# A four-layer gated attention and expert kernel: the first attention layer's scores in two rounded passes, key norms' roots by iteration on GpSimd

## The reference

```python
def _L0_xattn_ref(x_query, x_context, Wq, Wkv, Wp, bp, ln_g, ln_b):   # 16 heads of 16
    q, k = layernorm(q, ln_g, ln_b), layernorm(k, ln_g, ln_b)         # per head, over its 16
    q = q * SCALE
    attn = jax.nn.softmax(jnp.einsum('bhqd,bhkd->bhqk', q, k), axis=-1)
    out = jnp.einsum('bhqk,bhkd->bhqd', attn, v)
    ...
x = x + jnp.tanh(g_xattn[0]) * _L0_xattn_ref(_layernorm(x, axis=-1), ctx_1024, ...)
x = x + jnp.tanh(g_ffn[0]) * _L0_ffn_ref(_layernorm(x, axis=-1), ...)
x = x + jnp.tanh(g_xattn[1]) * _L1_xattn_ref(_layernorm(x, axis=-1), ctx_1024, ...)
x = x + jnp.tanh(g_ffn[1]) * _L1_ffn_ref(_layernorm(x, axis=-1), ...)
```

## Time and profile before

| | us |
|---|---|
| median of three runs (584.68 to 585.03) | 584.78 |
| the profiled execution: its own time | 583.47 |
| its span in the trace | 581.6 |
| PE / PEld busy in it | 555.4 / 477.1 |
| DVE / ACT / POOL busy in it | 408.8 / 319.4 / 271.9 |
| granted PE clock, mean | 0.995 |

### The profile page before, as it was taken

One profiled execution on the slowest core, in us unless ns is written; L12 is line 12 of the kernel. 1 busy time (PEld: TensorE's weight loads), 2 busy tenths in 40 slices (PEclk: granted clock), 3 DMA queues, 4 the chain that ended last, 5 costly groups with the idle time before them and its releaser, 6 DMA issues.

```text
span 581.6 us, 13614 instructions
## 1 busy us (share of the span) xinstructions
PE 555.4 (95%) x5542; PEld 477.1 (82%) x5542; DVE 408.8 (70%) x831; ACT 319.4 (55%) x632; POOL 271.9 (47%) x237
## 2 busy tenths in 40 slices
PE   8999999999989999999999999998999999999994
PEld 8776667677657878888888888877899999979994
DVE  7877568578696666777767867767677677746652
ACT  3554555555664665566555556654465656636641
POOL 3755655765740164657567465731203233421424
PEclk9999999999999999999999999999999999999998
DMA  8910840000000000000000000019374567726112
GB/s 259 357 45 2 318 194 3 1 3 2 2 2 1 2 1 2 8 9 17 18 9 18 10 25 1 25 26 414 91 253 149 170 213 253 259 32 236 28 20 26
DMA packets 24091, 50.92 MB, mean 88 GB/s; under 512 B 7072, under 2 KB 17104, under 8 KB 20688
## 3 DMA queue, kind: packets, MB, share of 16 engines
q1 hardware_dynamic: 18560, 45.20, 21.4%
q0 software_dynamic: 4224, 3.70, 3.6%
q10 hardware_dynamic: 1232, 1.01, 0.6%
HBM read 37.89 MB, written 13.31 MB: 88 GB/s over the span
## 4 chain that ended last, share of the span: by engine, by line
PE 81%; DVE 7%; ACT 5%; POOL 4%; issue 2%; DMA 1%; POOLq 0%; DVEq 0%; ACTq 0%
PE ps L59 15%; PE ps L60 14%; PE ps L61 14%; PE ps L607 5%; PE ps L750 4%; PE ps L625 4%; PE ps L768 4%; PE ps L738 4%; ACT P L1642 3%; DVE KN L1140 3%; PE ps L641 3%; PE ps L515 2%; PE ps L816 2%; POOL P L1947 2%; PE ps L522 2%
## 5 line engine op out<-in xcount | busy, mean ns | idle before, releaser
L1947 POOL TENSOR_SCALAR P<-P,rinv 112x487 f32<-112x487 f32 x56 | 88.2, 1588 | 50.9 <-DVE rinv L1183 50.7
L1140 DVE TENSOR_REDUCE KN<-ps 112x4 f32<-112x1500 f32 x32 | 55.0, 1719 | 28.7 <-PE ps L607 28.6
L424 POOL DMA_INDIRECT out<-WS,rows_i x16 | 28.7, 1791 | 92.5 <-ACT WS L1789 89.0
L60 PE MATMUL ps<-XGf,WH 128*128 128x256 f32 x252 | 71.3, 283 | 0.0
L61 PE MATMUL ps<-XGf,WL 128*128 128x256 f32 x252 | 71.3, 283 | 0.0
L59 PE MATMUL ps<-XGf,WH 128*128 128x256 f32 x252 | 71.3, 283 | 0.0
L1886 POOL TENSOR_TENSOR sr<-sv,mhalf 125x32 f32<-125x32 f32 x13 | 70.7, 5435 | 1.1
L1521 DVE TENSOR_TENSOR WL<-WR,WH 128x1024 fp32r<-128x1024 f32 x48 | 57.1, 1219 | 13.6 <-ACT WH L1843 10.0
L1642 ACT ACTIVATE P<-ps 125x1344 f32<-125x1344 f32 x32 | 41.3, 1292 | 32.8 <-PE ps L625 32.8
L1705 ACT ACTIVATE P<-ps,nm 112x487 f32<-112x487 f32 x64 | 41.9, 664 | 31.7 <-DVE nm L1175 31.7
L1843 ACT ACTIVATE WH<-WR 128x1024 fp32r<-128x1024 f32 x48 | 48.7, 1049 | 0.1
(11 more groups left out here) (290 smaller groups left out, 1546.1 us busy)
## 6 DMA issues: line engine op xcount, KB each, us to landing
WR<-in_gupT SPq DMA_DIRECT2D x16, 1024.0 KB, 7.2
WR<-in_dwnT SPq DMA_DIRECT2D x8, 1024.0 KB, 10.3
xs<-ZT SPq DMA_DIRECT2D x14, 516.0 KB, 6.0
CT<-in_ctxT SPq DMA_DIRECT2D x1, 2250.0 KB, 11.1
P<-xs SPq DMA_DIRECT2D x7, 256.0 KB, 10.8
P<-xs SPq DMA_DIRECT2D x9, 128.0 KB, 2.6
Wk<-in_L_xattn_Wk SPq DMA_DIRECT2D x2, 512.0 KB, 11.1
Wv<-in_L_xattn_Wv SPq DMA_DIRECT2D x2, 512.0 KB, 11.1
```

The costliest lines, as they stand in the source:

```text
L60: e.matmul(out, ah, bl, start=False, stop=False)
L1140: e.tensor_reduce(heads(KN[b % 2][0:NQ, 3, :])[:, 4 * k:4 * k + 4, 16], ps[0:NQ, 0:4, 0:NC], AX.X, ALU.max, negate=True).then_inc(s("smax" ...
L1947: e.tensor_scalar(P[:, k, 0:487], P[:, k, 0:487], rinv[:, k:k + 1], None, ALU.mult).then_inc(s("psc"), 1)
```

## The change

The first layer's keys and queries are split. The keys of a head have mean zero over their 16 numbers, so the sixteenth is dropped: the queries' sixteenth is taken off the other fifteen (`qg` on POOL, and on the shift `Bt` in `gain`), and a head's 32 columns in `KN` now hold 15 rounded keys, the one (column 15, before 16), and 15 numbers that are the rest of the keys. The query tile holds its 15 numbers twice. `ksc` scales the keys in place in `kraw` and writes the queries twice; the new stage `khi` (ACT) writes the rounded part, the new stage `klo` (DVE for batch 0, POOL otherwise) the rest. `KT`, `QA`, `QB` become FR; `spqc` becomes two steps, ACT's rounded copy and DVE's difference `QL0`. `S0` and `st` each run two passes, the rounded queries and then `QL0`, both over the same `KT`, of single-pass FR products. All three `spkc` copies are ACT's. The keys' power on POOL becomes fourteen small instructions (`key_roots`). The planned times of nearly every stage of the first layer and of `FIRST1`, `EVEN`, `PREP1`, `TAIL1` and `WEIGHTS` are others; `TQ` and the second layer's work are as they were.

```diff
-QUAD = ((-0.96, "S0"), (0.14, "max0"), (4.29, "qt2"), (4.68, "qt2c"), (7.69, "st"), (9.09, "ex"), (10.12, "V0"))
+QUAD = ((-0.51, "S0"), (-0.76, "max0"), (4.6, "qt2"), (4.96, "qt2c"), (7.69, "st"), (9.24, "ex"), (10.64, "V0"))
...
+PREP = ((-37.73, "cs"), (-48.02, "norm", 0), (-30.8, "kp", 1, 0), (-31.59, "xt", 0), (-31.68, "xtc", 0),
+        (-28.84, "kp", 1, 1), (-28.38, "kq", 1), (-27.41, "kss", 1), (-24.74, "kp", 0, 0), (-22.83, "kp", 0, 1),
+        (-21.5, "kq", 0), (-19.22, "kss", 0), (-16.99, "qg"), (-19.73, "ksc", 1), (-20.33, "khi", 1),
+        (-26.62, "klo", 1), (-16.17, "spk", 0), (-15.24, "spkc", 0), (-15.1, "spk", 1), (-14.26, "spkc", 1),
+        (-11.21, "ksc", 0), (-6.81, "khi", 0), (-11.53, "klo", 0), (-15.34, "qaff"), (-5.28, "spq"), (-4.56, "spqc"),
+        (-3.45, "spk", 2), (-3.79, "spkc", 2))
...
                 elif stage == "spk":
-                    w.wait_ge(s("ksc"), o_("ksc", b, 0 if j == 2 else 1))
+                    w.wait_ge(s(f"klo{0 if j == 2 else 1}"), b + 1)
...
-                    for g in range(4):
+                    for v, g in itertools.product(range(2), range(4)):
                         rows = slice(32 * g, 32 * g + 32)
-                        t = e.matmul(ps[0:NQ, g, 0:NC], QA[b % 2][rows, k * NQ:(k + 1) * NQ], KT[b % 2][rows, k, 0:NC],
-                                     start=True, stop=True, tile_position=(32 * g, 0))
+                        t = e.matmul(ps[0:NQ, g, 0:376], (QA, QL0)[v][b % 2][rows, k * NQ:(k + 1) * NQ],
+                                     KT[b % 2][rows, k, :], start=(v == 0), stop=(v == 1), tile_position=(32 * g, 0))
...
-                    for j, g in itertools.product(range(3), range(4)):
+                    for j, v, g in itertools.product(range(3), range(2), range(4)):
                         rows = slice(32 * g, 32 * g + 32)
                         t = e.matmul(ps[0:125, g, j * NQ:(j + 1) * NQ], KT[b % 2][rows, k, j * 125:(j + 1) * 125],
-                                     QB[b % 2][rows, k * NQ:(k + 1) * NQ], start=True, stop=True,
+                                     (QB, QL0)[v][b % 2][rows, k * NQ:(k + 1) * NQ], start=(v == 0), stop=(v == 1),
                                      tile_position=(32 * g, 0))
...
-                    e.tensor_tensor(out_, kraw[:, p, :].rearrange("p (h d) -> p h d", d=16),
-                                    sr[:, p, :].unsqueeze(2).to_broadcast([125, 32, 16]), ALU.mult).then_inc(s("ksc"), 1)
+                    n = 32 if p else 16
+                    k = kraw[:, p, 0:16 * n].rearrange("p (h d) -> p h d", d=16)
+                    t = e.tensor_tensor(k, k, sr[:, p, 0:n].unsqueeze(2).to_broadcast([125, n, 16]), ALU.mult)
+                    if p == 0:
+                        q = kraw[0:NQ, 0, 256:512].rearrange("p (h d) -> p h d", d=16)[:, :, 0:15]
+                        t = e.tensor_tensor(query_twice(b), q.unsqueeze(2).to_broadcast([NQ, 16, 2, 15]),
+                                            sr[0:NQ, 0, 16:32].unsqueeze(2).unsqueeze(3).to_broadcast([NQ, 16, 2, 15]),
+                                            ALU.mult)
+                    t.then_inc(s("ksc"), 1)
...
-                elif stage == "spkc" and i[1] != 2:
-                    keys_copy(e, w, *i)
+                elif stage == "spqc":
+                    b, = i
+                    w.wait_ge(s("spqa"), b + 1)
+                    e.tensor_tensor(QL0[b % 2], ps[:, bank("spq", b), 0:448], f_(QA[b % 2]),
+                                    ALU.subtract).then_inc(bank_sem("spq", b), 1)
...
+            q = query_twice(b)
+            e.tensor_tensor(q, q, Bt.rearrange("p (h d) -> p h d", d=16)[:, :, 0:15].unsqueeze(2).to_broadcast(
+                [NQ, 16, 2, 15]), ALU.add).then_inc(s("qaff"), 1)
...
+        def keys_low(e, w, b, p):
+            w.wait_ge(s("khi"), o_("khi", b, p))
+            e.tensor_tensor(keys_part(b, p, 1), keys_scaled(p), keys_part(b, p, 0),
+                            ALU.subtract).then_inc(s(f"klo{p}"), 1)
...
-                        w.wait_ge(s("ksc"), o_("ksc", b - 1, p))
+                        w.wait_ge(s(f"klo{p}"), b)
                     e.activation(sq[:, p, :], ps[0:125, bank("kp", b, p, 0), :], ACT.Square).then_inc(s("sq"), 1)
...
+                elif stage == "khi":
...
+                    e.activation(keys_part(b, p, 0).bitcast(FR), keys_scaled(p), ACT.Copy).then_inc(s("khi"), 1)
+                elif stage == "spkc":
+                    b, j = i
+                    w.wait_ge(s("spk"), o_("spk", b, j))
...
+                    e.activation(KT[b % 2][:, :, j * 125:(j + 1) * 125],
+                                 ps[:, bank("spk", b, j), 0:500].rearrange("p (g n) -> p g n", g=4),
+                                 ACT.Copy).then_inc(bank_sem("spk", b, j), 1)
...
+            for k in range(2):
+                e.tensor_copy(KT[k][:, :, NC:NC + 1], mhalf[:, 0:4].unsqueeze(2)).then_inc(s("pool0"), 1)
...
+                    q = q.rearrange("p (h d) -> p h d", d=16)
+                    e.tensor_tensor(q[:, :, 0:15], q[:, :, 0:15], q[:, :, 15:16].to_broadcast([NQ, 16, 15]),
+                                    ALU.subtract).then_inc(s("qg"), 1)
...
+                elif stage == "klo" and i[0]:
+                    keys_low(e, w, *i)
...
+        def key_roots(e, w, b, p):
+
+            v, y, u, sr_ = sv[:, p, :], sr[:, p, :], su[:, :], s("sr")
...
+            e.tensor_scalar(v, ss[:, p, :], 1.0 / 16, EPS, ALU.mult, ALU.add).then_inc(sr_, 1)
...
+            e.tensor_scalar(y.bitcast(I32), v.bitcast(I32), -0.5, 1597463007.0, ALU.mult, ALU.add).then_inc(sr_, 1)
+            k += 2
+            for _ in range(3):
+                w.wait_ge(sr_, k)
+                e.tensor_tensor(u, y, y, ALU.mult).then_inc(sr_, 1)
+                w.wait_ge(sr_, k + 1)
+                e.tensor_tensor(u, u, v, ALU.mult).then_inc(sr_, 1)
+                w.wait_ge(sr_, k + 2)
+                e.tensor_scalar(u, u, -0.5, 1.5, ALU.mult, ALU.add).then_inc(sr_, 1)
+                w.wait_ge(sr_, k + 3)
+                e.tensor_tensor(y, y, u, ALU.mult).then_inc(sr_, 1)
+                k += 4
```

168 lines of the change are left out of this document (84 added, 84 removed), and 13 rows, old and new, of the table FIRST.

## The result

The changed kernel takes 589.38 us (median of five, 587.24 to 589.67) against 584.78 of the kernel before: ratio 1.0071, 95% interval 1.0059 to 1.0082. It is slower by 0.7% where 1.6% faster was forecast, and outside the range. The profiled execution took 589.65 us with a span of 587.7 (before 583.47 and 581.6), with a mean granted clock of 0.979 (before 0.995).

A forecast was written before the change was run, and what follows sets the result against it. The prediction took the first layer's chain of `S0`, maximum, `st` and exponential as the bound, with PE nearly full. Loop -10.6, keys +0.5 and start +1.0 made -9.1 us: forecast 575.7 us, range 568.5 to 584.5.

The forecast's parts named there:

- the loop: First layer's quad loop: `S0` shorter by 0.28 us, `st` by 0.05, together 0.33 x 32 quads = -10.6 us.
- rival (a): `st` goes by columns, not weight loads, so single-pass data halves them: 8.6 us more gain, 567.1 us; chance 0.09.
- (d): Rival: float32r products in 32-row tiles run only two at a time, +0.72 us a quad: 609 us; chance 0.03.
- Planned times: New order of stages in both layers: changes the order only, taken as 0, bounds -3 and +3 us.
- Keys' preparation: Each batch's last key block: chain grows 1.4 us, covered by 2.6 us spare; +0.5 us for queues behind new waits.
- Start +1.0: Batch 0's chain to its first `S0`, without cover: added steps cost +1.0 us, bounds 0 and 2.5.
- Rival (b): Keys come late as POOL's small instructions are held up: at 0.5 us each, 582.0 us; chance 0.14.
- Rival (c): ACT's added copies, 2.2 us a batch, stand before the exponential and delay the loop: up to 591.1 us; chance 0.07.
- (e): Rival: no change, PE's other work sets the period; with the start's cost 585.3 us; chance 0.05.

The follow-up runs named there:

- before_roots: Kernel before, with only POOL's power for the keys' roots replaced by the iteration of small instructions: 585.18 us.
- power: Changed kernel with POOL's single power instruction again for the keys' roots: 596.44 us.
- first_two: Changed kernel with batch 1's last root and its scaling moved behind the second maximum, batch 0's first value product later: 587.10 us.
- start3: first_two, plus batch 1's first key scaling behind the third maximum and its query and last-key transposes behind `st` of quad 1: 586.46 us.
- start5: start3, plus batch 1's `khi` behind ACT's small copy of `st`'s operand, and every batch's context split 4.1 us later: 589.67 us.
- times_old: Changed kernel with all planned times of the kernel before, `khi` and `klo` right behind `ksc`: 618.90 us.
- hybrid: Changed kernel, meant to use the second layer's old tables only from batch 3, step 10; they replaced the new everywhere, giving steady's order: 590.18 us.
- steady: Changed kernel with the second layer's old tables for its repeating part (EVEN, ODD, PREP1, TAIL1, PAIRS2): 588.95 us.
- fill2: Changed kernel with extra transposes in PE's gaps at six places, the first group before `st` of quad 0: 586.83 us.
- best2: start5 and hybrid together, with extra transposes in PE's gaps: 587.25 us against 584.78 of the kernel before.
- best4: start3's and most of best3's moves, changed kernel's own second layer, third maximum before batch 1's scalings, some batch 2 key steps 5 us later: 590.96 us.
- best3: best2 with four ACT and weight-split entries moved, later context split for batch 2 only, and hybrid's cut as meant: 586.89 us.

## Why the prediction was wrong

The forecast was -9.1 us, the traces show +6.1. Of these 15.2 us the start makes 9.3 (+1.0 taken, +10.3 measured), quad 23 1.8 (+0.5 taken for late keys, +2.3 measured) and the second layer with what follows 4.8 (0 taken); the loop was 0.7 better than its term.

**The loop's steps were right.** `S0` 0.61 (forecast 0.62), `st` 0.87 (0.87); rival (a) is out, and so is (d): four float32r tiles do overlap, since two at a time would have made 0.96 of `S0`. The term itself was right in part by luck. Its -10.6 us was for 32 quads. The 27 periods of quads 3 to 23 and 24 to 31 would gain 8.9 us by it and gained 11.3. The two links did lose 0.34 us a quad as forecast; about 0.1 us more a quad is waiting between the links, for which there was no term.

**"Planned times: taken 0, bounds -3 and +3" failed**, and with it the whole frame of the sum. I costed the arithmetic part by part and took the order as something that could be set aside. It cannot: the same arithmetic in the old order takes 618.9 us, 29.5 more, where the bounds were 3 either way. PE's gaps of 8.8 us in the earlier trace rows say nothing on what an order for other durations and more stages is worth.

**"Keys' preparation +0.5, as 2.6 us of spare cover it" failed.** The 2.6 us were measured at one block of the old order. before_roots confirms it there and power refutes it in the changed kernel. The queue that I named ("on ACT, behind `khi`, the exponential") is where power loses its 1.0 us a batch. `key_roots` undisturbed is 4.54 us, not 4.2.

**Start +1.0 failed**, as +3.3 to quad 0 and +7.0 to quad 3. The way to quad 0 has three pieces. Batch 0's last sum of squares and the keys' first transposes, before and then after:

```profile
12.26 0.69 DVE L1109 TENSOR_REDUCE ss<-sq 125x32 f32<-125x512 f32 x1 [0.54 <-ACT sq L1609]
...
18.36 1.45 PE L586 MATMUL ps<-ident,KN 125*128 125x125 f32 x12
```

```profile
13.63 0.69 DVE L1117 TENSOR_REDUCE ss<-sq 125x32 f32<-125x512 f32 x1 [1.67 <-ACT sq L1628]
...
21.13 1.04 PE L590 MATMUL ps<-ident,KN 125*128 125x125 f32 x8 [2.10 <-DVE KN L1351]
```

The sum begins 1.4 us later, ahead of every added stage; from it to the transposes it is 7.5 us instead of 6.1, and from these to `S0` 3.6 instead of 3.1. So what lies behind that sum, the added steps above all, grew by 1.9 us where 1.0 was taken, inside the bounds of 0 to 2.5, and 1.4 are the order's. The early value product does not make them: with it put back, first_two has a PE gap of 1.2 us at 21 us instead of 2.1, but there the sum begins at 13.51 and quad 0 at 24.57, hardly earlier than 24.70.

Of the +7.0, 1.9 us lie between quads 1 and 2 (7.5 us, before 5.6): DVE makes batch 1's other root before it takes the second maximum, and first_two, which puts the root behind it, has 5.59. The third period is 5.5 us longer (10.9, before 5.4). For this one the trace gives the chain. POOL and DVE, changed kernel:

```profile
22.01 0.68 DVE L1117 TENSOR_REDUCE ss<-sq 125x32 f32<-125x512 f32 x1
...
27.55 0.74 POOL L1926 TENSOR_TENSOR kraw<-kraw,S 112x256 f32<-112x256 f32 x1 [4.55 <-ACT kraw L1629]
28.36 0.62 POOL L1929 TENSOR_TENSOR kraw<-kraw 112x240 f32<-112x240 f32 x1
29.07 0.22 POOL L2004 TENSOR_SCALAR sv<-ss 125x32 f32<-125x32 f32 x1
...
30.85 1.72 DVE L1156 TENSOR_REDUCE KN<-ps 112x4 f32<-112x1500 f32 x1
31.12 1.87 POOL L2011 TENSOR_TENSOR su<-sr 125x32 f32<-125x32 f32 x1
33.07 1.40 POOL L2013 TENSOR_TENSOR su<-su,sv 125x32 f32<-125x32 f32 x1
...
36.42 1.70 DVE L1136 TENSOR_TENSOR kraw<-kraw,sr 125x512 f32<-125x512 f32 x1 [2.07 <-POOL sr L2017]
```

and POOL before:

```profile
22.01 0.22 POOL L1882 TENSOR_SCALAR sv<-ss 125x32 f32<-125x32 f32 x1 [2.26 <-DVE ss L1109]
22.31 5.45 POOL L1886 TENSOR_TENSOR sr<-sv,mhalf 125x32 f32<-125x32 f32 x1
27.71 0.80 POOL L1893 TENSOR_TENSOR kraw<-kraw,S 112x256 f32<-112x256 f32 x1
```

Batch 1's first sum of squares is ready at 22.7 us, before at 21.9. Before, POOL took its root at once and the queries' gain (`qg` 1) after it. In the new order `qg` 1 stands first and waits 4.55 us for queries that come at 27.5; the root begins 7.1 us later, is then lengthened by 2.8 us, and DVE, ACT and PE are released in a row at 36.4, 38.2 and 39 us. The chain of waits of that stretch runs over just these instructions. power bears it out: its root takes 5.8 us here instead of 7.3, and its third period is 1.6 us shorter. In first_two, start3, start5 and power POOL stands still for the same 4.55 us: what I moved lay behind this, which is why each wait only changed its place. That a swap of `qg` 1 and `kss` 1 1 would mend it is argued from this chain and was not tried. So whether the changed arithmetic can beat the kernel before stays open.

**Rival (b) was right in kind, not in place.** It expected instructions held up and keys late in each batch; the hits that cost time are at 31 to 38 us and at quad 23. In between the 39 squares of POOL's iteration (L2011) have a median of 0.24 us; five of them took 0.8 to 1.9 us, and but for the first no longer period stands beside them. At quad 23, DVE and POOL:

```profile
146.39 2.10 POOL L1283 TENSOR_TENSOR KN<-KN,S 112x480 f32<-112x480 f32 x1
...
147.31 2.13 DVE L1255 SCALAR_TENSOR_TENSOR X<-tt,tg,X 112x256 f32<-112x256 f32 x1
```

L1255 has a median of 0.48 us, L1283 a least of 1.22. The Trainium skill (SBUF — State Buffer, "SBUF: two separate sides") says that of a VectorE operation with two SBUF inputs and a GpSimd operation the one that starts first has the shared port pair for the whole instruction. The trace agrees here as far as the end of L1283 at 148.49: L1255 was first held until then. It ended 0.95 us later instead of 0.48, with `klo` on POOL from 148.45 to 149.16; who held whom there the rows don't tell. The next maximum so began at 150.04 us, 1.5 us after its `S0` had ended, and PE waited 1.65 us for it. **Rival (c)** (copies before the exponential) is what power shows, not the changed kernel's steady quads.

**The second layer was left out of the sum** but for the word "order". Its +4.1 us is the new order: with the old one in times_old, and the same instructions, it is 189.0 us. 1.6 us lie behind its fifth score; the 2.5 before it are partly work that only stands on another side of the first score (one value product of 1.1 us). From quad 28 to the last score it is 222.4 against 218.9, and 220.5 in times_old.

**The clock was no term at all**, since every window of the earlier trace rows had it full. The changed kernel's trace has some 20 us at half clock in its first 181 us. Only 1.3 us of their price is read off directly, at quad 23, but the executions of one kernel tell more: first_two's shortest took 583.75 us at a mean granted clock of 0.988, its longest 590.48 at 0.973; hybrid's 587.79 at 0.982 and 592.17 at 0.970; the changed kernel's 587.24 at 0.984 and 589.65 at 0.979. That is 0.4 to 0.5 us for each thousandth; steady's (587.22 at 0.985, 590.74 at 0.974) give 0.3. fill2, which adds nothing but transposes, gains some 2.5 us. From 0.979 to the 0.995 of the kernel before these rates make 5 to 8 us, as much as the whole loss. This is an estimate from executions that differed by themselves, not a test, and it lies inside the rows of the table above, not beside them. best2 bounds it from the other side: its shortest execution, the traced one, has 0.993 and took 585.07 us, still no less than the 584.43 of the kernel before. So even with the clock nearly full the order takes back what the loop gains.

**One sum is off**: (e), no change with the start's cost of 1.0, is 585.8 us and not 585.3. No chance hangs on it.

## What to carry to other kernels

When a change comes with a new order, cost the order: walk the new list of each in-order engine at the start, where nothing is hidden, and ask of each stage what it waits for and who is queued behind it; one stage ahead of its time on POOL began a root 7.1 us late here. A slack measured in one order is no property of the work. And read the chain of waits from its far end: first_two, start3, start5 and best4 moved the last wait about, while the first one, 4.55 us of an engine that "is not the bottleneck", stood in the same chain. Look at the granted clock too: a new order that leaves PE short gaps can lose it, and here executions of one kernel lay up to 6.7 us apart with it.

## What was unexpected of the hardware

- PE's clock fell at about 33.8 us (worked out from the window's 0.72) after a gap of 1.9 us and within one of 1.2, with DVE, ACT and POOL at work all the while, and stayed at half for some 13.6 us with PE busy from 40 us on. It is not the same from run to run: the same gap of 1.65 us did and did not bring it. The kernels with such gaps spread accordingly: first_two's ten executions over 6.7 us, the kernel before's seven to nineteen per comparison over about 2.
- A small POOL instruction with two SBUF inputs took 1.87 us instead of 0.24, from 31.12 to 32.99, while DVE was first in a reduction out of PSUM (30.85 to 32.57) and only then in its two-input product (32.48 to 32.90). So it was held before that product began, with the product ready and queued. In best3 `qaff` took its undisturbed 1.22 us beside the same reduction, when DVE's next two-input instruction, a split, was still waiting for ACT (until 35.40). `klo`, which began at 35.51, after that wait but before the split's own start at 35.80, took 2.39 us instead of 0.71. In the changed kernel the square at 58.71 took 1.43 us beside a reduction that ended at 59.44 and a split that began at 59.36. All this was read from the rows and not tested apart.
- A POOL power does not hold DVE for its length: in the kernel before, DVE's two-input split has its usual length in the middle of one.

```profile
135.34 5.43 POOL L1886 TENSOR_TENSOR sr<-sv,mhalf 125x32 f32<-125x32 f32 x1
...
139.85 0.93 DVE L1070 TENSOR_TENSOR CS<-CT,CS 128x750 fp32r<-128x750 f32 x1
```

By the sentence of the Trainium skill above, "the whole instruction", it would have waited until 140.77.
